# Values of the wide-headed cross-attention computed two stages earlier and kept in DRAM, in a two-layer decoder kernel

## What is computed

```python
x = ln(x + linear_attention_exp(x))        # layer 0, 16 heads of 16
x = ln(x + cross_attention(x, ctx))        # 16 heads of 16, then an MLP
x = ln(x + routed_experts(x))              # 8 experts, top 2, capacity 140
x = ln(x + taylor_attention(x))            # layer 1, 16 heads, values of 64
x = ln(x + wide_cross_attention(x, ctx))   # 16 heads of 64
x = ln(x + self_attention_and_experts(x))
```

```python
q = (x @ w_q).reshape(B, SQ, 16, 64)
k = (cond @ w_k).reshape(B, SKV, 16, 64)
v = (cond @ w_v).reshape(B, SKV, 16, 64)   # depends on the text alone
attn = softmax(einsum('bqhd,bkhd->bhqk', q, k) * 64 ** -0.5)
out = einsum('bhqk,bkhd->bqhd', attn, v).reshape(B, SQ, 1024) @ w_out + b_out
```

## Time and profile before

| | us |
|---|---|
| median of 3 runs | 1503.38 |
| lowest, highest | 1493.66, 1509.24 |
| profiled execution, device time | 1492.97 |
| its span in the trace | 1491.1 |
| busy in the span: TensorE, VectorE, ScalarE, GpSimd | 1137.2, 723.0, 600.1, 300.4 |

### The profile page before, as it was taken

The page is one execution under the profiler, slowest core; times in us unless marked ns, Lnnn a source line. Parts: engine busy times, 40 slices in busy tenths (PEclk is TensorE's granted clock), DMA queues, the critical chain, the costliest instruction groups (busy, mean ns, idle before and its releaser), DMA issues.

```text
span 1491.1 us, 20688 instructions
## 1 busy us (share of the span) xinstructions
PE 1137.2 (76%) x8320; PEld 801.7 (54%) x8320; DVE 723.0 (48%) x1676; ACT 600.1 (40%) x1404; POOL 300.4 (20%) x308
## 2 busy tenths in 40 slices
PE   7987688766187737777778878878888577778996
PEld 4665466554087734545555555545555345554764
DVE  3323566416667637544535545545555455535303
ACT  4311266522056503332324534444454255447452
POOL 3311123200500052101111011101000705323453
PEclk9857689875599968886889989999999688777998
DMA  8400154004447240000023000000000000000000
GB/s 282 89 0 26 48 101 87 19 0 155 142 138 242 97 157 13 0 1 1 0 96 128 1 11 11 12 1 1 1 1 1 1 0 1 1 1 1 1 1 25
DMA packets 32752, 70.62 MB, mean 47 GB/s; under 512 B 8256, under 2 KB 22560, under 8 KB 28448
## 3 DMA queue, kind: packets, MB, share of 16 engines
q1 hardware_dynamic: 29888, 64.48, 14.4%
q0 software_dynamic: 1536, 3.67, 0.8%
q10 hardware_dynamic: 1232, 1.15, 0.3%
HBM read 60.19 MB, written 9.04 MB: 46 GB/s over the span
## 4 chain that ended last, share of the span: by engine, by line
PE 48%; DVE 27%; ACT 15%; POOL 5%; issue 3%; DMA 2%; SPq 0%; DVEq 0%; ACTq 0%; POOLq 0%
PE psum L344 39%; ACT s_p L2047 4%; DVE s_p L2099 3%; DVE s_k L2068 2%; POOL rs L2467 2%; DVE s_max L1115 2%; ACT sc L2347 2%; DVE s_max L2088 2%; PE psum L1003 2%; PE psum L975 2%; ACT s_k L2020 1%; DVE s_pT L2080 1%; DVE junk L1448 1%; DVE s_q L1767 1%; DVE wu L948 1%
## 5 line engine op out<-in xcount | busy, mean ns | idle before, releaser
L496 POOL TENSOR_TENSOR rstd<-meanvar,minus_half 112x1 f32<-112x1 f32 x40 | 23.2, 581 | 502.8 <-DVE meanvar L482 502.6
L2047 ACT ACTIVATE s_p<-psum,s_max 112x375 f32<-112x375 f32 x128 | 72.3, 569 | 103.6 <-DVE s_max L2088 103.5
L344 PE MATMUL psum<-ctx,Wk 128*128 128x375 f16 x320 | 64.1, 332 | 26.1 <-DVE s_k L2068 11.8
L2068 DVE SCALAR_TENSOR_TENSOR s_k<-psum,s_k 128x375 f16<-128x375 f32 x64 | 34.0, 547 | 95.7 <-ACT s_k L2020 95.7
L1115 DVE TENSOR_REDUCE s_max<-psum 112x2 f32<-112x750 f32 x64 | 60.0, 937 | 38.3 <-PE psum L975 37.5
L344 PE MATMUL psum<-x_ch,w_Wq 128*128 128x224 f32 x192 | 56.4, 426 | 14.4 <-DVE s_k L2068 8.8
L344 PE MATMUL psum<-Wv,ctx 128*125 128x512 f16 x240 | 62.2, 390 | 3.3 <-ACT s_v L2027 1.4
L456 PE MATMUL psum<-ident,x_tok 112*128 112x112 f32 x80 | 18.4, 328 | 60.2 <-DVE x_tok L491 56.8
L2088 DVE TENSOR_REDUCE s_max<-psum 112x1 f32<-112x375 f32 x128 | 63.7, 539 | 0.0
L1067 ACT ACTIVATE s_pT<-psum 125x672 f32<-125x672 f32 x64 | 46.8, 731 | 36.6 <-PE psum L991 35.3
L1987 PE MATMUL psum<-ident,s_p 112*125 112x112 f32 x384 | 56.1, 278 | 5.0 <-DVE s_p L2099 5.0
(11 more groups left out here) (352 smaller groups left out, 2820.2 us busy)
## 6 DMA issues: line engine op xcount, KB each, us to landing
raw_wg<-in_wg SPq DMA_DIRECT2D x8, 1024.0 KB, 4.9
raw_wu<-in_wu SPq DMA_DIRECT2D x8, 1024.0 KB, 5.5
raw_wd<-in_wd SPq DMA_DIRECT2D x8, 1024.0 KB
ctx_raw<-in_ctxT SPq DMA_DIRECT2D x16, 375.0 KB, 3.2
s_kd<-k_halves SPq DMA_DIRECT2D x48, 93.8 KB, 3.8
k_halves<-s_k SPq DMA_DIRECT2D x8, 375.0 KB, 3.2
w_Wv<-in_Wv SPq DMA_DIRECT2D x2, 1024.0 KB, 9.7
w_Wo<-in_Wo SPq DMA_DIRECT2D x2, 1024.0 KB, 11.7
```

Of the source, the lines that this page charges most:

```text
L344: ins = TE.matmul(bank, left, right, start=i == 0, stop=last)
L2047: SC.activation(rings["p4"][2 * n + j], rings["s4"][(n, j)][0:N, 0:S], ACT.Exp, bias=s4_max[b % 2][:, h:h + 1], accum_out=s4_sum[b % 2][:, ...
L2068: VE.scalar_tensor_tensor(s4_k[b % 2][:, t, 1, :], rings["misc4"][unit][:, 0:S], 1 / WSCALE, s4_k[b % 2][:, t, 0, :], ALU.mult, ALU.subtra ...
```

## The change

The 48 value units of the wide cross-attention move out of stage 4. A unit (`v4`) is now: five matmuls, ScalarE's copy to one of four staging tiles `s2_v` (125 rows x 512), and an SP put (`vput`) into a DRAM tensor in two transfers, of 112 and 13 rows. 28 of them are placed in stage 2: six after `prob2`, one after batch 3 and batch 7 of each round of counting, three ahead of each half of expert 1's splitting. The other 20 are a stream of stage 3, one per round from its start. In stage 4 each half of a batch (8 heads) is fetched back (`vget`, again 112 and 13 rows) into one of three tiles. `Wv4` is loaded and split in stage 1.

The text halves are made by GpSimd once, in stages 0 and 1, and put out to DRAM, each put behind the next raw load (`cput`); for the values and again for the keys they are fetched (`cget`) in place of being computed.

Loads: `g_w3` goes out at expert 4; expert 1's first matrix after the logits, the other two after the first six value units; `g_w4` after the last normalisation of stage 3's input. The expert results have eight buffers; the first four fetches are placed at the end of stage 2, and the first four combines rest for 7 to 10 times `REST` (1500 ns of placed cost).

```diff
+    spent_w = Region(nc, wts.base, 30 * KB)
+    Wv4_16 = spent_w.tensor("Wv4_16", [P, 4, HW], F16)
+    spent_w.restart(16 * KB)
+    s2_v = [spent_w.tensor(f"s2_v{i}", [SCH, HW // 2])[:] for i in range(4)]
+    vx = nc.dram_tensor("values4", [B, 2, NCH, SCH, HW // 2], F32)
+    V_ROWS = (slice(0, N), slice(N, SCH))
+    VUNITS = [(b, c, j) for b in range(B) for c in range(NCH) for j in range(2)]
+    L_vput = [results(f"dma_v_put{i}", 16) for i in range(4)]
+    L_vget = [results(f"dma_v_get{i}", 16) for i in range(3)]
...
+    L_cput = [results(f"dma_ctx_put{i}", 16) for i in range(3)]
+    L_cget = [results(f"dma_ctx_get{i}", 16) for i in range(3)]
+    cx = nc.dram_tensor("text_halves", [B, P, 3 * S], F16)
...
+    value_units = iter(VUNITS)
+
+    def values(count, s):
+
+        for b, c, j in itertools.islice(value_units, count):
+            for name in (None, ("vput", b, c, j)):
+                L_vput[VUNITS.index((b, c, j)) % 4].plan(name)
+            v4_stage[b, c, j] = s
+            yield [("v4", s, b, c, j), ("vput", b, c, j)] + (
+                ctx_units(B + b + 3) if (c, j) == (NCH - 1, 1) else [])
+
+    def place_values(count, s):
+        for units in values(count, s):
+            for unit in units:
+                place(unit)
+
+    v4_stage = {}
+
+    def place_ctx(i):
+
+        for unit in ctx_units(i):
+            place(unit)
+
+    def ctx_units(i):
+        if i < B:
+            return [("ctx", i)] + [("cput", i - 1)] * (i > 0)
+        return [("cput", B - 1)] * (i == B) + [("cget", i)] * (i < 3 * B)
+
+    def ctx_at(i):
+        return G["ctx", i] if i < B else L_cget[i % 3]["cget", i]
...
+        if what == "v4":
+            s, b, c, j = at
+            ring = rings[f"values{s}"]
+            pe.wait_ge(V["wv4",], ctx_at(B + b), *ring.free(unit))
+            mm(ring[unit][0:SCH, :], [(ctx16[(B + b) % 3][:, t, c * SCH:(c + 1) * SCH],
+                                       Wv4_16[:, w, j * 512:(j + 1) * 512])
+                                      for t, w in CTX_PRODUCTS], T.up("v4", *at))
...
+        if what == "v4":
+            s, b, c, j = at
+            u = VUNITS.index((b, c, j))
+            if u >= 4:
+                act.wait_ge(L_vput[u % 4]["vput", *VUNITS[u - 4]])
+            act.wait_ge(T["v4", *at])
+            SC.activation(s2_v[u % 4], rings[f"values{s}"][unit][0:SCH, :], ACT.Copy,
+                          scale=1 / WSCALE).then_inc(*A.up("v4", *at))
...
-                pool.wait_ge(*ctx_spent(i - 3))
+                pool.wait_ge(*ctx_spent(i - 3), L_cput[i % 3]["cput", i - 3])
...
+        elif what == "vput":
+            b, c, j = at
+            u = VUNITS.index((b, c, j))
+            sp.wait_ge(A["v4", v4_stage[b, c, j], b, c, j])
+            for rows in V_ROWS:
+                SY.dma_start(vx[b, j, c, rows, :], s2_v[u % 4][rows]).then_inc(
+                    *(L_vput[u % 4].up("vput", b, c, j) if rows.start else L_vput[u % 4].up()))
+        elif what == "cput":
+            i, = at
+            sp.wait_ge(G["ctx", i])
+            SY.dma_start(cx[i, :, :], ctx16[i % 3][:].rearrange("p t n -> p (t n)")).then_inc(
+                *L_cput[i % 3].up("cput", i))
+        elif what == "cget":
+            i, = at
+            sp.wait_ge(*ctx_spent(i - 3), L_cput[i % B % 3]["cput", i % B])
+            if i - 3 < B:
+                sp.wait_ge(L_cput[i % 3]["cput", i - 3])
+            SY.dma_start(ctx16[i % 3][:].rearrange("p t n -> p (t n)"), cx[i % B, :, :]).then_inc(
+                *L_cget[i % 3].up("cget", i))
...
+        if i < B:
+            return T["v1", i, NCH - 1], T["k1", keys_stage(i), i, KC - 1]
+        return (T["v4", v4_stage[i - B, NCH - 1, 1], i - B, NCH - 1, 1],) if i < 2 * B else (T["k4", i - 2 * B, HW // P - 1],)
...
     for i in range(3):
-        place(("ctx", i))
+        place_ctx(i)
...
+    step("wv4in")
+    step("wv4", "A wv4, V +2, V wv4")
+    g_wv4 = Group("dma_wv4")
+    Wv4 = g_wv4.load(work, "Wv4", [P, 2, HW])
...
-        if b + 3 < 2 * B:
-            place(("ctx", b + 3))
+        place_ctx(b + 3)
...
+        place(("wv4in",))
+        yield from until(("st1", 6 * HP - 1))
+        yield [("wv4",)]
...
+    rings["values2"] = rings["mx2"]
+    step("v4", "T v4, A v4", "values#", "A v4", 1280)
+    step("get")
+    L_get = [results(f"dma_get{i}", 16) for i in range(B)]
+    got_w = Region(nc, ringm.base + 30 * KB, 16 * KB)
+    got = [got_w.tensor(f"got{i}", [N, 2, D]) for i in range(B)]
...
     place(("logits2",))
+    place(("load", 1, 0))
     place(("prob2",))
+    place_values(6, 2)
+    place(("load", 1, 1))
+    place(("load", 1, 2))
     for x in range(3):
         place(("turn2", x))
...
+            if b % 4 == 3:
+                place_values(1, 2)
...
         for half in range(2):
+            place_values(3, 2)
             split_expert(1, j, half)
...
+        if e == 4:
+            place(("w3in",))
...
+    for b in range(4):
+        place(("get", b))
...
+    def gpsimd_get(b):
+        pool.wait_ge(L_eout[0]["eout", E0 - 2], L_eout[1]["eout", E0 - 1])
+        for k in range(2):
+            GP.indirect_dma_start(
+                got[b][:, k, :], None, eout[:, :],
+                bass.IndirectOffsetOnAxis(get_i[:, k, b:b + 1], axis=0)
+                ).then_inc(*L_get[b].up("got", b, k))
...
     def sync_s2():
         fence(sp, 2)
-        g_w3.start()
-        for j, (n, _, _) in enumerate(MATS):
-            SY.dma_start(raw[j][:], a[n][1]).then_inc(*L_exp[j].up("expert", 1, j))
         for what, *at in plans[2]:
-            if what == "load":
+            if what == "w3in":
+                g_w3.start()
+            elif what == "load":
                 e, j = at
                 sp.wait_ge(A["hi", e - 1, j, 1], V["lo", e - 1, j, 1])
...
+    spent_w.restart(8 * KB)
     Wk4 = g_w4.load(spent_w, "Wk4", [P, 2, HW])
-    Wv4 = g_w4.load(spent_w, "Wv4", [P, 2, HW])
     Wk4_16 = ringm.tensor("Wk4_16", [P, 4, HW], F16)
-    Wv4_16 = ringm.tensor("Wv4_16", [P, 4, HW], F16)
...
+    rings["misc2"], rings["values3"] = rings["misc3"], rings["y3"]
+    step("w4in")
...
     def s3_combine(b):
         yield from until(("get", b))
-        yield from rest(2 * REST)
+        yield from rest((7 + b) * REST if b < 4 else 2 * REST)
         yield [("combine", 2, b)]
-        if b + 2 < B:
-            place(("get", b + 2))
+        if b + 4 < B:
+            place(("get", b + 4))
         yield from norm_and_turn(2, b)
...
     def s3_split():
-        for j in range(2):
-            yield from until(("y3", j, 3))
-            yield [("split4", j)]
-
-    for b in range(B):
-        L_get[b % NG].plan(("got", b, 0))
-        L_get[b % NG].plan(("got", b, 1))
-    place(("get", 0))
-    place(("get", 1))
-    place(("wo3",))
-    weave(*(follow(s3_combine, range(j, B, 4)) for j in range(4)),
+        place(("wo3",))
+        yield from until(("norm", 2, B - 1))
+        place(("w4in",))
+        yield from until(("y3", 3, 3))
+        yield [("split4",)]
+
+    weave(values(None, 3), *(follow(s3_combine, range(j, B, 4)) for j in range(4)),
           follow(s3_out, range(0, B, 2)), follow(s3_out, range(1, B, 2)),
...
-        pool.wait_ge(L_eout[0]["eout", E0 - 2], L_eout[1]["eout", E0 - 1])
         for what, *at in plans[3]:
             if what == "get":
-                b, = at
-                if b >= NG:
-                    pool.wait_ge(V["got", 2, b - NG])
-                for k in range(2):
-                    GP.indirect_dma_start(
-                        got[b % NG][:, k, :], None, eout[:, :],
-                        bass.IndirectOffsetOnAxis(get_i[:, k, b:b + 1], axis=0)
-                        ).then_inc(*L_get[b % NG].up("got", b, k))
+                gpsimd_get(*at)
...
-    s4_v = [work.tensor(f"s4_v{j}", [SCH, NCH, H // 2, DHW]) for j in range(2)]
+    s4_v = [work.tensor(f"s4_v{j}", [SCH, NCH, H // 2, DHW]) for j in range(3)]
...
+        place_ctx(2 * B + b + 3)
...
-    def s4_values(b, j):
-        if b:
-            yield from until(("av4", (b - 1) * HP + j * 4 + 3))
-        for c in range(NCH):
-            yield [("v4", b, j, c)]
-        if j:
-            yield from until(("k4", b, HW // P - 1))
-            if b + 3 < B:
-                place(("ctx", B + b + 3))
+    def s4_values(m):
+        if m >= 3:
+            yield from until(("av4", 4 * (m - 3) + 3))
+        yield [("vget", m)]
...
-                    yield from until(("v4", o // HP, o % HP // 4, NCH - 1))
+                    yield from until(("vget", o // 4))
...
+    for m in range(2 * B):
+        L_vget[m % 3].plan(None)
+        L_vget[m % 3].plan(("vget", m))
+    weave(s4_heads(), follow(s4_values, range(2 * B)),
...
-                pe.wait_ge(V["w4", 0], g_w4.ready, G["ctx", B + b], *rings["misc4"].free(unit))
+                pe.wait_ge(V["wk4",], ctx_at(2 * B + b), *rings["misc4"].free(unit))
                 mm(rings["misc4"][unit][:, 0:S],
```

(36 more changed lines are left out.)

73 lines of the change are left out of this document (43 added, 30 removed).

## The result

The changed kernel takes **1458.84 us** (median of 4 runs, 1458.30 to 1463.44). The kernel before, timed beside it, takes 1499.23 us (4 runs, 1493.66 to 1509.24). The ratio is 0.973, with a 95% interval of 0.9669 to 0.9792: faster, by 2.7%. I had forecast 1431 with a range of 1397 to 1468. The time lies in the range, but 28 us above the forecast and outside the forecast's own 1415 to 1447; it is next to the 1457 of rival (a), and the range holds it only because rivals (a) and (b) had widened it.

The account below looks back on a forecast made before the run. The prediction took TensorE to set stage 4, with hollow stretches in routing and the fetch. Its terms, -78 + 1 + 5 + 0 = -72 us, gave 1431 us from the median of 1503.38, range 1397 to 1468.

Parts of the forecast that it names:

- rival (a): Stage 4: only the value units' work goes, pairs then wait for VectorE's key and softmax operations; 1457 us, chance 0.18.
- Rival (b): Routing and fetch gaps: the moved units run at the low clock and behind full DMA engines; 1452 us, chance 0.13.
- Part 1: Stage 4 without the value units: 78 us shorter, with ends of 52 and 99.
- 9.69 falls to 3.9: Ordinary stage 4 batch: the pair of heads where TensorE waits for ScalarE's value copy, 5.8 us saved.
- 7.13 to 3.9: Ordinary stage 4 batch: a later pair of heads loses its value units, 3.2 us saved.
- 8.33 less two units: Ordinary stage 4 batch: the pair that also holds the output product loses two units' work, 2.2 us saved.
- free GpSimd: 0: Stage 4: fetching the text halves instead of computing them frees GpSimd, gaining 0 because nobody waited for it.
- Part 3: Routing: value units cost +1 us behind the logits, 0 in counting, +5 in the hole before the first expert.
- Part 2: Values fetched back from DRAM in stage 4 stay covered, cost 0; splitting the value weights in stage 1, net 0.
- Rival (d): Stage 4: value fetches come late and TensorE waits at each half-batch; 1527 us at 6 us each, chance 0.04.
- Part 4: Fetch of expert results and stage 3, taking the 20 other units: net 0, ends -6 and +9 us.
- Rival (c): Stage 4 falls to VectorE's own sum, 21 us more saved; 1410 us, chance 0.07.

Follow-up runs that it names:

- Experiment 1: In stage 4 ScalarE copies the transposed rows right behind their transposition: on the changed kernel 1425.92 us (0.9521), on the kernel before 1470.53 us (0.9824).
- experiments 3: The changed kernel with the early stage 4 row copy and expert 2's loads behind the inputs of experts 0 and 1: 1418.22 us, ratio 0.9455.
- experiment 6: Changed kernel with early row copy, expert 2's loads after the first expert's transposition, expert inputs before the last six routing value units, seven staging buffers: 1416.61 us.
- experiment 7: Changed kernel with early row copy, expert 2's loads behind the inputs, and value-weight split after stage 1's last transposition of probabilities: 1416.48 us, ratio 0.9447.
- experiment 2: The changed kernel with expert 2's three weight loads issued behind the inputs of experts 0 and 1: 1448.93 us, ratio 0.968.

## Why the prediction was right or wrong

**Part 1, stage 4: direction and place right, the size off by 33 of 78 us.** The opening did what was said: rounds of 2.98 us, 31.6 us from the first product to the first scores before and 25.0 after, -6.6 for the 6.5 forecast. Batch 0 gave 2.6, not 9: only three value units stood between its scores, not six, and one of them in a pair that kept its 3.9 us without it. Batches 1 to 5 gave 28.9 (242.2 to 213.3 us), not 56. Batch 6 gave 3.6, not 6.5. Batch 7, of which I had said nothing, gave 2.9: the last three value units stood in it. The five add up to the 44.6. Of batches 1 to 5 the one that turned out worst is the second with queries: 49.03 us before, 48.89 after.

The step that failed is "9.69 falls to 3.9"; my own sign, no pair over 6.5 us outside the query rounds, fails at 8.55. I read the 1.90 us wait for ScalarE's copy of values in the earlier trace rows as what made that pair long, and took pairs with two key units (3.85) as its measure. But those pairs have both banks of misc4 and this one has one: the transposed rows sit in the other. The row was there in the trace of before (a wait of 0.94 us for x_ch, 4.7 in all), small because value units waited in front of it. With them gone the same bank holds up the keys for 3.11 us, the 9.69 becomes 8.55, and the pair before it goes from 3.42 to 5.74. In a batch with queries, for which I took the same gain, the bank is held longer still (20.3 us for 14.9), and the two pairs take 29.9 us where they took 29.3. Experiment 1 shows the cause by moving nothing but the copy: 8.82 for the two pairs, of which the second takes the forecast's 3.80, and 33 us in all. With the bank freed in both kernels the change shortens stage 4, measured as in the table, from 353.0 to 301.1 us, by 52 (46 to 49 with the stage 4 of experiments 3, 6 and 7, 304.1 to 307.4): at most the 52 of the work, and no stalls on top. So the second step, that a unit costs more than its work because its stalls go with it, was wrong too: "7.13 to 3.9" and "8.33 less two units" came true, but the pair of 9.69 and those with queries gave less than the work of their units.

A term that I had put at nothing is in this gain as well. The two pairs behind the output product hold no value unit in either kernel and still went from 3.46 to 2.90 and from 3.34 to 2.69. In the kernel before GpSimd makes the text halves beside them (L513 to L518), and VectorE's two scalings take longer there than a pair later:

```profile
1018.34 0.90 POOL L516 TENSOR_TENSOR ctx<-ctx_raw,ctx 128x375 f16<-128x375 f32 x1
1019.32 0.90 POOL L518 TENSOR_TENSOR ctx<-ctx_raw,ctx 64x375 f16<-64x375 f32 x1
```

```profile
1019.85 1.39 DVE L2099 TENSOR_SCALAR s_p<-s_p,s_sum 112x375 f32<-112x375 f32 x2
...
1023.18 0.74 DVE L2099 TENSOR_SCALAR s_p<-s_p,s_sum 112x375 f32<-112x375 f32 x2
```

In the later batches of that kernel, which make no text halves, the second of these pairs takes 2.68 to 2.69 already. So my "free GpSimd: 0" should have been some 0.65 us in each of four batches, an estimate of under 3 us from these rows; no run tests it.

**Rival (a), only the work goes,** comes nearest: 1457, and 44.6 us in stage 4 where it has 52. That its number is met is in part luck, for its reason is not the one: the waits for VectorE's keys fell in total (21.9 to 14.9), and the waits that took the place of that for ScalarE's copy of values are again for ScalarE, for its copies of the rows (4.7 to 14.0) and of the attention's output (0.6 to 8.0).

**Part 3, routing: the chain right, its size too low.** Behind the logits +0.9 for +1: six units in 9.07 us, for which I had 8.6. The hole +8.6 for +5, by the chain as it was told: puts behind loads on SyncE, evictions behind the puts, the inputs' issue behind these. Two of my signs of being wrong came true here: TensorE's wait before the transposition is 16.00 us, not under 8, and ScalarE waits 13.7 us for landed puts there (18.5 with those of stage 3), not under 5. The windows 407 to 413 and 419 to 426 show 343 GB/s at 0.94 and 344 at 0.97: the DMA engines are nearly full there, and moving 3 MB out of the hole gives 7.1 us back (experiment 2). The order of the issues counts as well: experiment 6 takes another 5 us off the hole with the same bytes. Rival (b) in its strong form is false: nineteen units in a row took 20.72 us, 1.09 each. The granted clock was 1.00 from 389 to 407 over that stream, which cycles through eight banks. The Trainium skill's warning on psum-queue depth-cycling (TensorE: Matmul & The Clock Gate) is about such matmuls with small idles between the groups. The stream had none (TensorE busy 6.00 of 6 us from 395 to 407), so its case did not arise here.

**Part 2, the fetches: right in its price, too hopeful in its margin.** Stage 4 starts at 788 now, and SyncE's queue reaches the first fetch at 797, 9 us in. The loads before it and the first three fetches keep the engines at 0.98 and 340 GB/s (788 to 813), where I had taken 380, and they are idle only from about 821 (share 0.69 from 818, 0.04 from 821), 33 us in, where I had the first values at 23. TensorE's first product with values stands at 824.58, with no wait. So the cover at the first fetches was some 4 us, not the 11 from 794 to 805. TensorE waits for none, and leaving 13 of 16 out changes nothing. Rival (d) is false, with 125 rows too: there it is the puts that cost, not the fetches.

**Part 4 and the split of the weights: right within what can be told.** Fetch and stage 3 -0.8 for 0; from the first fetch to the first transposition 17.2 us where there were 20.9, for the 4 less of the forecast. The split moved to stage 1 costs nothing that experiment 7 can find.

**Rival (c)** needed pairs at VectorE's sum. After the change an ordinary batch takes 37.4 us and with the early copy 32.6, where that sum with its small operations was 28. It was not reached.

The sum by its own steps: -44.6 where -78 stood, +8.6 for +5, +0.9 for +1, 0 for 0, so -35 instead of -72 on the profiled stretches. The spans differ by only 29.5, with the +6.4 of stage 1 in them; the medians, measured together, by 40.4. The profiled execution of the changed kernel was the slowest of its four.

## What to carry to other kernels

When work is taken away beside a stall, ask of every shared buffer how long each of its users holds it, not who is named as the last releaser: a bank filled by one instruction and emptied 8.5 to 20 us later, where the emptying engine's order has it, cost 25 to 33 us in both kernels, and was hidden behind a wait for something else. Price a removed unit at its own work, and count its stalls only if the buffer they wait for has no other late user. Look at the number of rows of each DMA before the number of DMAs.
